# Layer 0's attention rebuilt: q and k in two float32r pieces, heads in four groups of 32 partitions, projections between the batches

## Chip, cores and metric

One core of one Trainium2 chip runs the whole two-layer block as one program. The metric is the device time of one execution in microseconds; the figure of the kernel before is the median of three runs.

## The reference, cut to what matters

There are 16 batches of 128 features by 256 positions. Only the first of the four blocks, layer 0's cross attention, is touched by the change. It has 16 heads of 8 features.

```
q = split(Wq @ layernorm(x) + bq)   k = split(Wk @ ctx + bk)   v = split(Wv @ ctx + bv)   # 16 heads of 8
scores = q^T k / sqrt(128)          attn = softmax(scores over the keys)                  # 256 x 256 for each head
x = x + tanh(g_xattn[0]) * (Wo @ (attn v) + bo)
```

The routed experts, the mLSTM, the second attention and its experts follow and need all 16 batches of x.

## The kernel before

Each engine has its instruction list written out by hand, and semaphores order them. In `layer0_*` the work on one head is two square score tiles: a maximum pass with the query on the partitions (`score_max`, L204, reduced by DVE at L423) and an exponential pass with the key on the partitions (`exponentials`, L232, ACT's exponential at L340). The negated maxima of a batch reach the second pass as extra rows of the contraction: PE turns them to rows, ACT and POOL split them, and SP copies them with a DMA into rows of `qs` (`max_rows`, L153).

Accuracy comes from q and k split in three bfloat16 pieces. All nine products of pieces stand below each other: 9 x 8 = 72 contraction rows, 75 with the maximum's three. SP builds that stack for a batch by storing the pieces in DRAM (`store_parts`, L132) and reading them back once for each product (`stack`, L146 and L147), into a ring of four batches (`A_RING`).

All projections, the split and the stores come first, for all 16 batches. Then 28 heads (`AHEAD`) of maxima run, and then a loop in which PE alternates maxima of head i + 28 with exponentials of head i. After every four heads (a group) `times_v` (L246) multiplies by v for four heads side by side, ACT copies the sums (L348), PE transposes them back (L256) and DVE divides (L430, L434). After a batch come two transposes, the output projection (L270), ACT's bias (L369) and DVE's add into x (L451). Banks: two for maxima, two for exponentials, two for `times_v`, one for the turn back, one for the batch's end.

SP's list is in order. In the main loop `stack(b + 4)` waits until the exponentials of batch b have been issued, and `max_rows(b + 2)` stands behind it:

```
        if n % A_PAIRS == A_PAIRS - 1 and n // A_PAIRS + A_RING < NB:
            stack(n // A_PAIRS + A_RING)
```

Of the kernel before, what the change touches and what calls it, by code (L numbers as in the profile page):

```python
# [11 lines left out]
ALU = mybir.AluOpType  # L12
# [61 lines left out]
QPART = (0, 0, 0, 1, 1, 1, 2, 2, 2)  # L74
KPART = (0, 1, 2, 0, 1, 2, 0, 1, 2)
TERM_ROWS = len(QPART) * HD
MAX_ROWS = 3
ROWS = TERM_ROWS + MAX_ROWS
TILES = 4
GROUPS = HEADS // TILES  # L80
A_PAIRS = HEADS // 2
A_SLOTS = 3
A_RING = 4
A_EXPS = 8
AHEAD = HEADS + 3 * HEADS // 4
A_STEPS = NB * A_PAIRS + 6


def layer0_memory(k, stack):
    sb = tensors(k, stack, "a")  # L90
    m = namedtuple("m", "wqT wkT wvT woT bias normed vaug whole parts qs ks negmax mrow mparts expo inv outq sumT outT proj stats mean_var rstd")
    return m(
        sb("wqT", [P, P]), sb("wkT", [P, P]), sb("wvT", [P, P]), sb("woT", [P, P]), sb("bias", [P, 4]),
        sb("normed", [P, NB, D]), sb("vaug", [P, NB, 2, HEADS, HD + 1]),
        [sb(f"whole{i}", [P, 2, BANK]) for i in range(A_SLOTS)], [sb(f"parts{i}", [P, 2, 3, BANK], BF16) for i in range(A_SLOTS)],
        [sb(f"qs{i}", [ROWS, HEADS, POS], BF16) for i in range(A_RING)], [sb(f"ks{i}", [96, HEADS, POS], BF16) for i in range(A_RING)],
        [sb(f"negmax{i}", [P, HEADS, 2]) for i in range(2)], [sb(f"mrow{i}", [32, P]) for i in range(2)],
        [sb(f"mparts{i}", [32, 3, P], BF16) for i in range(2)], [sb(f"exp{i}", [P, 2, POS]) for i in range(A_EXPS)],
        [sb(f"inv{i}", [P, 2, TILES]) for i in range(2)], [sb(f"outq{i}", [P, 2, HEADS, HD]) for i in range(2)],
        [sb(f"sumT{i}", [P, POS]) for i in range(2)], [sb(f"outT{i}", [P, POS]) for i in range(2)], [sb(f"proj{i}", [P, POS]) for i in range(2)],  # L100
# [4 lines left out]
def layer0_semaphores(k):  # L105
    s = k.sems("a", "weights_in var root normed qk_sums v_sums qk_whole qk_rounded q_rest k_rest q_middle k_middle q_low k_low v_copied k_ones "
               "max_scores maxed max_turned max_copied max_split exp_scores exped cleared weighted sums_copied turned_back divided "
               "out_sums out_turned proj_sums projected added")
    return s, {n: [k.sem(f"a_{n}{i}") for i in range(count)] for n, count in (("q_out", A_SLOTS), ("k_out", A_SLOTS), ("stack_in", A_RING), ("max_in", A_RING))}


def layer0_sp(k, m, s, ring):
# [7 lines left out]

    load_inputs(0)
    sp.dma_start(k.gates[:, :], io["gates"]).then_inc(k.gates_in, DMA)
    for dst, name in ((m.wqT, "a_wqT"), (m.wkT, "a_wkT"), (m.wvT, "a_wvT"), (m.woT, "a_woT"), (m.bias, "a_bias")):
        sp.dma_start(dst[:, :], io[name]).then_inc(s.weights_in, DMA)
    for chunk in range(1, NCHUNK):
        load_inputs(chunk)

    def store_parts(i):
        for n, (name, ready) in enumerate((("q", s.q_low), ("k", s.k_low))):
            sp.wait_ge(ready, i + 1)  # L130
            for j in range(2):
                sp.dma_start(io[f"a_{name}_parts"][2 * i + j].rearrange("t p n -> p t n"),  # L132
                             m.parts[i % A_SLOTS][:, n, :, j * POS:(j + 1) * POS]).then_inc(ring[f"{name}_out"][i % A_SLOTS], DMA)

    def stack(b):
        r, i = b % A_RING, b // 2
        flat = lambda t, first, count: t[first * HD:(first + count) * HD, :, :].rearrange("p h n -> p (h n)")
        parts_of = lambda n: io[f"a_{n}_parts"][b].rearrange("t (d h) n -> t d (h n)", d=HD)
        sp.wait_ge(ring["q_out"][i % A_SLOTS], 2 * DMA * (i // A_SLOTS + 1))
        sp.wait_ge(ring["k_out"][i % A_SLOTS], 2 * DMA * (i // A_SLOTS + 1))  # L140
        if b < A_RING:
            sp.wait_ge(s.k_ones, b + 1)
        else:
            sp.wait_ge(s.exp_scores, (b - A_RING + 1) * HEADS)
        for t in range(3):
            sp.dma_start(flat(m.qs[r], 3 * t, 3), parts_of("q")[t].unsqueeze(0).broadcast_to([3, HD, HEADS * POS])).then_inc(ring["stack_in"][r], DMA)  # L146
            sp.dma_start(flat(m.ks[r], 3 * t, 3), parts_of("k")).then_inc(ring["stack_in"][r], DMA)  # L147

    def max_rows(b):
        sp.wait_ge(s.max_split, b + 1)  # L150
        for part in range(MAX_ROWS):
            row = TERM_ROWS + part
            sp.dma_start(m.qs[b % A_RING][row:row + 1, :, :].rearrange("o h (q n) -> o (h q) n", q=2),  # L153
                         m.mparts[b % 2][:, part, :]).then_inc(ring["max_in"][b % A_RING], DMA)

# [2138 lines left out]
```

## Time and profile before

| | |
|---|---|
| median of 3 runs | 1817.8 us (1807.99 to 1822.12) |
| profiled execution | 1817.43 us, span 1816.1 us, mean granted clock 0.94 |
| layer 0's attention | 0 to 350.4 us of the span |
| PE, DVE, ACT, POOL busy in the span | 88%, 69%, 56%, 42% |
| DMA moved | 137.42 MB, mean 76 GB/s |

The busy shares are means over stages with different limits. The changed stage is the first fifth of the span; the stages behind it start when its last batch has been added to x.

### The profile page before, as it was taken

How to read it: one execution, taken by the hardware profiler on the slowest of the kernel's cores; microseconds unless marked ns; L12 is line 12 of the kernel's file. 1: busy time of each engine (PE TensorE's matmuls, PEld its weight loads, DVE VectorE, ACT ScalarE, POOL GpSimd, SP SyncE). 2: the span in 40 equal slices, each digit the busy share in tenths (PEclk: the TensorE clock that was granted, in tenths of full speed). 3: DMA queues.
4: the chain of work that ended last, by engine and by line, in shares of the span. 5: the costliest groups of instructions: out<-in, count | busy, mean ns of one | idle time of the engine just before them, and what ended most of it. 6: DMA issues, size and time to landing. Idle time of an engine off the chain costs nothing.

```text
span 1816.1 us, 30483 instructions
## 1 busy us (share of the span) xinstructions
PE 1606.5 (88%) x10932; PEld 1268.4 (70%) x10932; DVE 1259.6 (69%) x2321; ACT 1019.4 (56%) x2050; POOL 765.8 (42%) x575
## 2 busy tenths in 40 slices
PE   4379999789999999999986964899899999999898
PEld 2135555368888888888872533788787778888687
DVE  6458788378644455444445576999999999999454
ACT  4247777644433335333335653877776877677453
POOL 5200000024435333333330014798798688877000
PEclk9569899899999999999996987999999999999899
DMA  5613232243343333343400002123112111211220
GB/s 155 154 55 83 76 84 61 80 111 105 94 129 106 104 110 102 108 116 102 118 10 6 4 2 92 48 72 103 56 56 68 56 56 56 68 48 30 70 47 24
DMA packets 73349, 137.42 MB, mean 76 GB/s; under 512 B 12824, under 2 KB 41308, under 8 KB 70384
## 3 DMA queue, kind: packets, MB, share of 16 engines
q1 hardware_dynamic: 73200, 135.48, 26.4%
q8 instruction: 88, 1.44, 0.3%
q14 instruction: 61, 0.50, 0.1%
HBM read 125.70 MB, written 8.95 MB: 74 GB/s over the span
## 4 chain that ended last, share of the span: by engine, by line
PE 54%; DVE 19%; issue 9%; DMA 8%; ACT 6%; POOL 2%; SPq 1%; DVEq 0%; ACTq 0%; POOLq 0%
PE bank L67 13%; PE bank L69 13%; PE bank L68 13%; DMA a_qs<-a_mparts 5%; DVE b_straight L1938 3%; DVE b_straight L1892 2%; PE bank L246 2%; PE bank L232 2%; PE bank L204 2%; ACT b_turned L1809 2%; DVE b_peak L1909 2%; POOL e_hidden L944 1%; DVE b_probs L1907 1%; PE bank L1700 1%; PE bank L1732 1%
## 5 line engine op out<-in xcount | busy, mean ns | idle before, releaser
L944 POOL TENSOR_TENSOR e_hidden<-e_gated,e_comb_wide 128x512 f32<-128x512 f32 x132 | 211.0, 1599 | 346.7 <-DVE e_gated L909 331.1
L784 ACT CAST e_hidden_hi<-e_hidden 128x512 fp32r<-128x512 f32 x132 | 82.0, 622 | 320.6 <-POOL e_hidden L944 320.6
L902 DVE TENSOR_TENSOR e_hidden_lo<-e_hidden,e_hidden_hi 128x512 fp32r<-128x512 f32 x132 | 98.2, 744 | 209.8 <-ACT e_hidden_hi L784 209.8
L423 DVE TENSOR_REDUCE a_negmax<-bank 128x2 f32<-128x512 f32 x256 | 165.6, 684 | 64.6 <-PE bank L204 63.3
L69 PE MATMUL bank<-e_x_hi,e_weights_lo 128*128 128x512 f32 (+1 forms) x528 | 209.5, 397 | 0.0
L67 PE MATMUL bank<-e_x_hi,e_weights_hi 128*128 128x512 f32 (+1 forms) x528 | 208.4, 395 | 0.7 <-ACT e_comb_rows L744 0.7
L68 PE MATMUL bank<-e_x_lo,e_weights_hi 128*128 128x512 f32 (+1 forms) x528 | 208.4, 395 | 0.0
L1809 ACT ACTIVATE b_turned<-bank,b_swap_bias 64x512 f32<-64x512 f32 x256 | 174.9, 683 | 17.7 <-PE bank L69 12.9
L1996 POOL TENSOR_TENSOR b_turned<-b_turned,b_rope 128x512 f32<-128x512 f32 x128 | 167.5, 1329 | 5.3 <-ACT b_turned L1809 4.8
L340 ACT ACTIVATE a_exp<-bank 128x512 f32<-128x512 f32 x256 | 142.9, 596 | 42.8 <-PE bank L232 35.4
L69 PE MATMUL bank<-e_weights_hi,e_hidden_lo 128*128 128x256 f32 (+1 forms) x528 | 149.4, 283 | 0.0
L67 PE MATMUL bank<-e_weights_hi,e_hidden_hi 128*128 128x256 f32 (+1 forms) x528 | 148.2, 281 | 0.5 <-DVE e_hidden_lo L902 0.5
L68 PE MATMUL bank<-e_weights_lo,e_hidden_hi 128*128 128x256 f32 (+1 forms) x528 | 148.4, 281 | 0.0
L1938 DVE TENSOR_TENSOR b_straight<-b_straight,b_turned 128x512 f32<-128x512 f32 x128 | 140.5, 1136 | 0.0
L1798 ACT ACTIVATE b_probs<-b_probs,b_peak_scaled 128x128 f32<-128x128 f32 x256 | 99.7, 391 | 68.2 <-DVE b_peak_scaled L1911 68.1
L204 PE MATMUL bank<-a_ks,a_qs 72*128 72x256 bf16 x512 | 108.0, 297 | 31.0 <-DMA a_ks<-a_k_parts 13.2
L1978 POOL TENSOR_TENSOR b_qk_lo<-b_raw_qk,b_qk_hi 128x512 fp32r<-128x512 f32 x64 | 84.7, 1324 | 109.9 <-DVE b_qk_hi L1872 109.9
L909 DVE TENSOR_TENSOR e_gated<-e_silu,bank 128x512 f32<-128x512 f32 x132 | 90.5, 686 | 56.7 <-PE bank L69 44.2
L232 PE MATMUL bank<-a_qs,a_ks 75*128 75x256 bf16 x512 | 100.2, 280 | 21.0 <-DMA a_qs<-a_mparts 20.1
L69 PEld LDWEIGHTS bank<-e_x_hi,e_weights_lo 128*128 128x128 f32 (+1 forms) x528 | 98.7, 187 | 22.7
L67 PE MATMUL bank<-b_x_hi,b_qk_hi 128*128 128x512 f32 x256 | 103.0, 402 | 12.8 <-POOL b_qk_lo L1978 4.5
L67 PEld LDWEIGHTS bank<-e_x_hi,e_weights_hi 128*128 128x128 f32 (+1 forms) x528 | 99.4, 188 | 19.7 <-ACT e_comb_rows L744 1.1
(326 smaller groups left out, 4318.1 us busy)
## 6 DMA issues: line engine op xcount, KB each, us to landing
e_comb_wide<-e_combT SPq DMA_DIRECT2D x130, 256.0 KB, 4.0
e_raw<-in_e_weights SPq DMA_DIRECT2D x64, 384.0 KB, 4.5
b_raw_qk<-in_b_wqk SPq DMA_DIRECT2D x64, 256.0 KB, 2.8
a_qs<-a_q_parts SPq DMA_DIRECT2D x48, 192.0 KB
a_ks<-a_k_parts SPq DMA_DIRECT2D x48, 192.0 KB
b_raw_v<-in_b_wv SPq DMA_DIRECT2D x16, 512.0 KB, 3.8
b_raw_o<-in_b_wo SPq DMA_DIRECT2D x64, 128.0 KB, 2.0
moe_comb_wide<-b_comb_rows SPq DMA_DIRECT2D x16, 256.0 KB, 6.7
```

Source lines behind the costliest of these rows:

```text
L67: pe.matmul(out, w_hi, x_hi, start=start, stop=False, skip_group_check=True)
L68: pe.matmul(out, w_hi, x_lo, start=False, stop=False, skip_group_check=True)
L69: return pe.matmul(out, w_lo, x_hi, start=False, stop=stop, skip_group_check=True)
L204: last = pe.matmul(bank[:, qb * POS:(qb + 1) * POS], m.qs[r][0:TERM_ROWS, h, qb * P:(qb + 1) * P], m.ks[r][0:TERM_ROWS, h, :], start=True, ...
L232: last = pe.matmul(bank[:, kb * POS:(kb + 1) * POS], m.ks[r][0:ROWS, h, kb * P:(kb + 1) * P], m.qs[r][0:ROWS, h, :], start=True, stop=True)
L340: act.activation(m.expo[at % A_EXPS][:, :, :].rearrange("p k q -> p (k q)"), banks[2 + h % 2][:, :], ACT.Exp, scale=float(1 / np.sqrt(np.f ...
L423: dve.tensor_reduce(m.negmax[b % 2][:, h, :], banks[h % 2][:, :].rearrange("p (q n) -> p q n", q=2), AX.X, ALU.max, negate=True).then_inc( ...
L944: pool.tensor_tensor(m.hidden[i][0:rows, :], m.gated[i][0:rows, :], m.comb_wide[u % E_RING][0:rows, chunk * BANK:(chunk + 1) * BANK], ALU. ...
L1798: last = act.activation(w.probs[n % 3][:, b, :], w.probs[n % 3][:, b, :], ACT.Exp, scale=SCALE, bias=w.peak_scaled[i][:, b:b + 1], accum_o ...
L1809: last = act.activation(w.turned[i][dst:dst + half, which, :], banks[bank][src:src + half, :], ACT.Identity, bias=m.swap_bias[dst:dst + ha ...
L1938: dve.tensor_tensor(w.straight[n % 2][:, which, :], w.straight[n % 2][:, which, :], w.turned[n % 2][:, which, :], ALU.add).then_inc(s.rotated)
L1996: pool.tensor_tensor(x, x, w.rope[:, 1, :].unsqueeze(1).to_broadcast([P, CHUNK, S]), ALU.mult).then_inc(s.qk_sine)
```

## The change

- q and k become two float32r pieces (high, low) instead of three of bfloat16, and three products are kept: 24 contraction rows, 26 with two rows for the maximum. Heads are stacked in four groups (lanes) of 32 partitions, four heads in each; a matmul then uses 32 partitions of the array.
- Work is counted in slots of two heads; a batch is 8 slots, a pair of batches 16. One DVE instruction reduces both heads of a slot over two banks (1024 elements). The exponentials follow the maxima by `LEAD` = 15 slots (30 heads). Order on PE in a slot: exponential, maximum, exponential, three maxima, two exponentials.
- Only the first two pairs are projected ahead; the others are projected in slots 0, 2 and 4 of a pair (q, k, v), in banks of the maxima's ring (`USES`). The projections lose one ACT pass, the second rounding pass and POOL's passes: ACT writes the high piece, DVE the low one.
- Stores and stacks are made for a pair of batches at a time: six stores and eight stack DMAs. The ring holds three pairs. `stack(i)` for i of 3 and more waits for the exponentials of pair i - 3.
- POOL splits the maxima before the transpose, ACT copies the rows, SP places them with two DMAs.
- `times_v` and the turn back have one bank each, and the batch's end shares the bank of the turn back. ACT's bias pass at the end is gone: POOL adds the bias to x, and DVE adds the product from PSUM. The tanh of the gates and their load come later in the order.

```diff
-MAX_ROWS = 3
+A_TERMS, MAX_ROWS = 3, 2
+TERM_ROWS = A_TERMS * HD
 ROWS = TERM_ROWS + MAX_ROWS
+LANE, LANES = 32, 4
+TILES = LANES
+A_SLOTS = HEADS // 2
+A_PAIRS = NB // 2
+A_RING, A_PARTS, A_MAXIMA, A_EXPS = 3, 2, 4, 8
+LEAD = 15
+A_LAST = NB * A_SLOTS
+A_STEPS = A_LAST + LEAD + A_SLOTS
+TURN_AT, SPLIT_EVERY = A_SLOTS + 2, 2 * A_SLOTS
+SCORE_SLOTS = 2
+EXP_BANK, SUM_BANK, TURN_BANK = 4, 6, 7
...
+    i, at = t // SPLIT_EVERY + 2, t % SPLIT_EVERY
+    return ({0: "q", 2: "k", 4: "v"}[at], i) if at in (0, 2, 4) and i < A_PAIRS else None
...
+    uses = [(kind, i) for kinds in ("qk", "v") for i in range(2) for kind in kinds]
+    for t in range(A_LAST):
+        uses.append(("max", t))
+        if projection_of(t):
+            uses.append(projection_of(t))
+    return uses
...
+    def store(i):
+        sp.wait_ge(s.low, 2 * (i + 1))
+        both = lambda n, part: m.parts[i % A_PARTS][:, n, part, :].rearrange("p (j n) -> p j n", j=2)
+        for n, (dst, terms) in enumerate(((k.q_stack, (0, 0, 1)), (k.k_stack, (0, 1, 0)))):
+            for term, part in enumerate(terms):
+                sp.dma_start(dst[2 * i:2 * i + 2, term].rearrange("j p n -> p j n"), both(n, part).bitcast(F32)).then_inc(ring["stored"][i % A_PARTS], DMA)
+    def stack(i):
+        r = i % A_RING
+        sp.wait_ge(ring["stored"][i % A_PARTS], 2 * A_TERMS * DMA * (i // A_PARTS + 1))
+        if i < A_RING:
+            sp.wait_ge(s.ones, A_RING)
+        else:
+            sp.wait_ge(s.exp_scores, (i - A_RING + 1) * 2 * HEADS)
+        for src, dst in ((k.q_stack, m.qs), (k.k_stack, m.ks)):
+            for lane in range(LANES):
+                rows = src[2 * i:2 * i + 2].rearrange("j t (d g h) n -> t d g j (h n)", g=LANES, h=GROUPS)[:, :, lane].rearrange("t d j n -> (t d) j n")
+                sp.dma_start(dst[r][LANE * lane:LANE * lane + TERM_ROWS, :, :, :].rearrange("p j h n -> p j (h n)").bitcast(F32),
+                             rows).then_inc(ring["stack_in"][r], DMA)
+    def max_rows(b):
+        sp.wait_ge(s.max_copied, b + 1)
+        for part in range(MAX_ROWS):
+            rows = m.qs[b // 2 % A_RING][TERM_ROWS + part:P:LANE, b % 2, :, :].rearrange("g h n -> g (h n)").bitcast(F32)
+            sp.dma_start(rows, m.mrow[b % 2][LANE * part:LANE * (part + 1), :].bitcast(F32)).then_inc(ring["max_in"][b % A_MAXIMA], DMA)
     load_inputs(0)
...
+    for t in range(A_STEPS):
+        at, i = t % SPLIT_EVERY, t // SPLIT_EVERY + 2
+        if t % A_SLOTS == TURN_AT % A_SLOTS and TURN_AT <= t < A_LAST + TURN_AT:
+            max_rows((t - TURN_AT) // A_SLOTS)
+        if at == 5 and i < A_PAIRS:
+            store(i)
+        if at == 9 and i < A_PAIRS:
+            stack(i)
 
 
...
+    def freed(use):
+        at = USE[use] - SCORE_SLOTS
+        if at >= 0:
+            kind, i = USES[at]
+            if kind == "max":
+                pe.wait_ge(s.maxed, i + 1)
+            elif kind == "v":
...
+    def scores(t):
+        u = t - LEAD
+        maximum, exponential = t < A_LAST, 0 <= u < A_LAST
+        if exponential:
+            if u % A_SLOTS == 0:
+                b = u // A_SLOTS
+                pe.wait_ge(ring["max_in"][b % A_MAXIMA], MAX_ROWS * DMA * (b // A_MAXIMA + 1))
+            if u:
+                pe.wait_ge(s.exped, 2 * u - 1)
+            exp_pair(u, 0, 0)
+        if maximum:
+            if t % (2 * A_SLOTS) == 0:
+                i = t // (2 * A_SLOTS)
+                pe.wait_ge(ring["stack_in"][i % A_RING], 2 * LANES * DMA * (i // A_RING + 1))
+            freed(("max", t))
+            max_pair(t, 0, 0)
+        if exponential:
+            exp_pair(u, 0, 1).then_inc(s.exp_scores)
+        if maximum:
+            max_pair(t, 1, 0)
+            max_pair(t, 0, 1)
+            max_pair(t, 1, 1).then_inc(s.max_scores)
+        if exponential:
+            if u:
+                pe.wait_ge(s.exped, 2 * u)
+            exp_pair(u, 1, 0)
+            exp_pair(u, 1, 1).then_inc(s.exp_scores)
...
+    def turn_back(g):
+        b, h = divmod(g, GROUPS)
+        pe.wait_ge(s.sums_copied, g + 1)
+        if g:
+            pe.wait_ge(s.divided, g)
+        if b and h == 1:
+            pe.wait_ge(s.out_turned, b)
+        if b and h == 2:
+            pe.wait_ge(s.added, b)
...
+    def to_features(b):
+        pe.wait_ge(s.divided, min(GROUPS * (b + 1) + 1, GROUPS * NB))
...
+        pe.wait_ge(s.divided, min(GROUPS * (b + 1) + 2, GROUPS * NB))
+        pe.matmul(banks[TURN_BANK][:, 0:POS], m.woT[:, :], m.outT[b % 2][:, :], start=True, stop=True).then_inc(s.proj_sums)
...
+    for t in range(A_STEPS):
+        u = t - LEAD
+        scores(t)
+        if projection_of(t):
+            project(*projection_of(t))
+        if t % A_SLOTS == TURN_AT % A_SLOTS and TURN_AT <= t < A_LAST + TURN_AT:
+            max_to_rows((t - TURN_AT) // A_SLOTS)
+        if u % 2 == 0 and 2 <= u < A_LAST + 2:
+            times_v((u - 2) // 2)
+        if u % 2 and 3 <= u < A_LAST + 3:
+            turn_back((u - 3) // 2)
+        if u % A_SLOTS == 4 and u >= 12:
+            to_features(u // A_SLOTS - 1)
+        if u % A_SLOTS == 6 and u >= 14:
+            residual(u // A_SLOTS - 1)
...
+    def high(kind, i):
+        n = "qk".index(kind)
+        act.activation(m.parts[i % A_PARTS][:, n, 0, :], banks[score_bank((kind, i))][:, :], ACT.Identity, bias=m.bias[:, n:n + 1]).then_inc(s.high)
...
+    def maxima(t):
+        b = t // A_SLOTS
+        (lane, h), _ = heads_of(t)
+        first = score_bank(("max", t))
+        dve.wait_ge(s.max_scores, t + 1)
+        if b >= 2 and t % A_SLOTS == 0:
+            dve.wait_ge(s.max_split, b - 1)
+        dve.tensor_reduce(m.negmax[b % 2][:, lane:lane + 2, h, :], k.psum[:, first:first + 2, :].rearrange("p s (q n) -> p s q n", q=2), AX.X, ALU.max,
                           negate=True).then_inc(s.maxed)
...
+    def divide(g):
+        b, h = divmod(g, GROUPS)
+        view = banks[TURN_BANK][:, 0:2 * P].rearrange("p (q g d) -> p q g d", q=2, g=LANES)
+        dve.wait_ge(s.turned_back, g + 1)
...
+    for t in range(A_STEPS):
+        u = t - LEAD
+        if t < A_LAST:
+            maxima(t)
+        if t and projection_of(t - 1):
+            read(*projection_of(t - 1))
+        if u % 2 == 0 and 4 <= u < A_LAST + 4:
+            divide((u - 4) // 2)
+        if u % A_SLOTS == 7 and u >= 15:
+            b = u // A_SLOTS - 1
+            dve.wait_ge(s.proj_sums, b + 1)
+            dve.wait_ge(s.biased, b + 1)
+            dve.scalar_tensor_tensor(k.resid[:, b, :], banks[TURN_BANK][:, 0:POS], k.gates[:, 0:1], k.resid[:, b, :], ALU.mult, ALU.add).then_inc(s.added)
...
-        pool.wait_ge(s.max_copied, b + 1)
-        pool.tensor_tensor(m.mrow[i][:, :], m.mrow[i][:, :], m.mparts[i][:, 0, :], ALU.subtract).then_inc(own.tick())
+        negmax, (high, low) = m.negmax[b % 2][:, :, :, :].rearrange("p g h q -> p (g h q)"), (m.mparts[b % 2][:, part, :] for part in range(2))
+        pool.wait_ge(s.maxed, A_SLOTS * (b + 1))
+        if b >= 2:
...
+        pool.tensor_scalar(k.resid[:, b, :], k.resid[:, b, :], m.late_bias[:, 0:1], None, ALU.add).then_inc(s.biased)
```

## Rows read from the trace of the kernel before

**Rows 1.** Windows of layer 0's attention: engines' busy us (instructions), granted clock, DMA share, GB/s.
```profile
0.00:66.00 66.00, 29.35 (x100) 17.14 (x100) 37.82 (x80) 30.36 (x54) 32.07 (x24) 0.85 0.54 157
66.00:111.00 45.00, 16.40 (x56) 3.91 (x57) 20.44 (x32) 2.81 (x5) 4.68 (x6) 0.50 0.43 114
111.00:118.00 7.00, 7.00 (x41) 3.84 (x42) 3.46 (x5) 4.08 (x9) 1.11 (x3) 0.50 0.00 0
118.00:126.00 8.00, 8.00 (x80) 4.87 (x79) 6.62 (x14) 6.34 (x13) 0.00 (x0) 0.98 0.03 5
126.00:322.00 196.00, 185.91 (x1861) 111.08 (x1860) 156.10 (x330) 151.03 (x316) 14.50 (x39) 0.97 0.29 76
322.00:350.50 28.50, 24.27 (x221) 10.77 (x219) 6.58 (x24) 21.34 (x47) 1.11 (x3) 0.94 0.01 2
```

**Rows 2.** The chain of waits, 60 to 360 us: start, length, what.
```profile
96.28 14.61 DMA a_qs<-a_mparts
...
163.29 7.34 DMA a_qs<-a_mparts
```

**Rows 3.** Timeline of the attention's last instruction: start, length, engine, line.
```profile
349.93 0.48 DVE L451 SCALAR_TENSOR_TENSOR resid<-a_proj,gates,resid 128x256 f32<-128x256 f32 x1 [3.05 <-ACT a_proj L369]
```

**Rows 4.** Timeline of SP's DMA issues for one batch: start, length, issue.
```profile
154.34 0.75 SPq L146 DMA_DIRECT2D a_qs<-a_q_parts  x1
155.13 0.44 SPq L147 DMA_DIRECT2D a_ks<-a_k_parts  x1
...
162.05 1.19 SPq L153 DMA_DIRECT2D a_qs<-a_mparts  x2
```

**Rows 5.** Windows of three DMA stretches: columns as in the first group.
```profile
38.00:40.00 2.00, 1.94 (x9) 0.93 (x7) 0.98 (x2) 2.00 (x4) 1.27 (x2) 1.00 1.02 286
76.00:84.00 8.00, 2.42 (x8) 0.52 (x8) 3.22 (x6) 0.00 (x0) 0.00 (x0) 0.50 0.77 144
163.00:169.00 6.00, 6.00 (x65) 3.67 (x65) 5.07 (x13) 5.00 (x11) 0.00 (x0) 1.00 0.20 71
```

**Rows 6.** Groups of instructions, 110.9 to 350.5 us: count, busy us, mean ns, idle before.
```profile
L423 DVE TENSOR_REDUCE a_negmax<-bank 128x2 f32<-128x512 f32 x227 | 146.9, 684 | 50.0 <-PE bank L204 50.0
L340 ACT ACTIVATE a_exp<-bank 128x512 f32<-128x512 f32 x256 | 142.9, 596 | 42.8 <-PE bank L232 35.4
...
L348 ACT COPY a_sumT<-bank 128x256 f32<-128x256 f32 x64 | 23.8, 372 | 26.1 <-PE bank L246 26.1
...
L434 DVE TENSOR_TENSOR a_outq<-bank,a_inv 128x64 f32<-128x64 f32 x64 | 14.4, 225 | 2.2
L430 DVE RECIPROCAL a_inv<-bank 128x8 f32<-128x8 f32 x64 | 12.7, 199 | 17.2 <-PE bank L256 17.2
...
L451 DVE SCALAR_TENSOR_TENSOR resid<-a_proj,gates,resid 128x256 f32<-128x256 f32 x16 | 7.8, 484 | 6.6 <-ACT a_proj L369 6.6
```

**Rows 7.** Groups of DVE's instructions in later stages, shapes kept apart.
```profile
L1948 DVE SCALAR_TENSOR_TENSOR b_outT_lo<-bank,b_head_bias,b_outT_hi 128x512 fp32r<-128x512 f32 x64 | 47.2, 737 | 3.5 <-ACT b_outT_hi L1837 3.5
...
L1344 DVE TENSOR_REDUCE m_factor<-m_square 128x64 f32<-128x1024 f32 x4 | 4.8, 1210 | 0.0
```

**Rows 8.** Timeline of PE, one group of four heads.
```profile
120.31 1.05 PE L246 MATMUL bank<-a_exp,a_vaug 128*9 128x256 f32 x16
121.29 0.39 PE L204 MATMUL bank<-a_ks,a_qs 72*128 72x256 bf16 x2
121.52 0.39 PE L232 MATMUL bank<-a_qs,a_ks 75*128 75x256 bf16 x2
```

**Rows 9.** Timeline of PE in the mLSTM stage: matmuls of 32 partitions each.
```profile
1037.01 1.17 PE L1236 MATMUL bank<-columns,m_keys 32*128 32x128 f32 x32
```

**Rows 10.** Timeline of PE in the expert stage: float32r matmuls of 256 columns.
```profile
471.71 0.28 PE L68 MATMUL bank<-e_weights_lo,e_hidden_hi 128*128 128x256 f32 x1
471.82 0.28 PE L69 MATMUL bank<-e_weights_hi,e_hidden_lo 128*128 128x256 f32 x1
```

**Rows 11.** Timeline of a projection of 512 columns in the first stretch.
```profile
35.40 1.02 PE L186 MATMUL bank<-ctx,a_wkT 128*128 128x512 f32 x2
```

More of the change, by code:

```diff
@@ L124, in layer0_sp @@
         sp.dma_start(dst[:, :], io[name]).then_inc(s.weights_in, DMA)
+    sp.dma_start(k.gates[:, :], io["gates"]).then_inc(k.gates_in, DMA)
     for chunk in range(1, NCHUNK):
         load_inputs(chunk)
[L128 to L154, printed above, removed]
-    for i in range(1, NB // 2 + 1):
-        store_parts(i - 1)
-        if i == 3:
-            stack(0)
-    for b in range(1, A_RING):
-        stack(b)
-    for i in range(AHEAD):
-        if i >= 2 and (i - 2) % HEADS == HEADS - 1:
-            max_rows((i - 2) // HEADS)
@@ L165, in layer0_sp @@
[L165 to L171 removed]
+    for i in range(2):
+        store(i)
[5 more added lines that the diff above has]
+        if at == 5 and i < A_PAIRS:
+            store(i)
+        if at == 9 and i < A_PAIRS:
+            stack(i)
@@ new lines, in layer0_act @@
+    for chunk in range(1, NCHUNK):
+        root(chunk)
+    act.wait_ge(k.gates_in, DMA)
+    act.activation(k.gates[:, :], k.gates[:, :], ACT.Tanh).then_inc(k.gates_ready)
+    for t in range(A_STEPS):
+        u = t - LEAD
+        if t and projection_of(t - 1) and projection_of(t - 1)[0] in "qk":
+            high(*projection_of(t - 1))
+        if 0 <= u < A_LAST:
+            exponentials(u)
+        if t % A_SLOTS == TURN_AT % A_SLOTS and TURN_AT <= t < A_LAST + TURN_AT:
+            max_to_rows((t - TURN_AT) // A_SLOTS)
+        if u % 2 == 0 and 2 <= u < A_LAST + 2:
+            times_v((u - 2) // 2)
+        if u % A_SLOTS == 4 and u >= 12:
+            to_features(u // A_SLOTS - 1)
@@ new lines, in layer0_dve @@
+    norm_start(0)
+    dve.memset(m.vaug[:, :, :, :, HD], 1.0)
+    dve.memset(banks[SUM_BANK][:, :], 0.0).then_inc(s.cleared)
+    norm_end(0)
+    for kind, i in USES[:4]:
+        read(kind, i)
+    for chunk in range(1, NCHUNK):
+        norm_start(chunk)
+        if chunk == 1:
+            for i in range(2):
+                read("v", i)
+    for chunk in range(1, NCHUNK):
+        norm_end(chunk)
+    dve.wait_ge(s.weights_in, 5 * DMA)
+    dve.wait_ge(k.gates_ready, 1)
+    dve.tensor_tensor(m.late_bias[:, :], m.bias[:, 3:4], k.gates[:, 0:1], ALU.mult).then_inc(s.late_bias)
```

377 lines of the change are left out of this document (127 added, 250 removed).

## The prediction

> **What bounds the kernel now.** I read the windows first, to cut the attention out of the span: it ends at 350.4 us, and nothing behind it starts before [rows 1, 3]. So the change is worth what it moves that end. The stretches differ. To 66 us everything is projected, split and stored. From 66 to 111 us PE is 36% busy, at half its clock. The chain shows why: the first exponential needs the first rows of maxima, whose DMA landed 14.61 us after its issue, at 110.9 us [rows 2]. From 111 us the loop of two heads runs, with PE at 95%, DVE at 80% and ACT at 77% of 126 to 322 us [rows 1]. A group of four heads is 3.3 us from one `times_v` to the next where nothing is late, and PE takes 0.98 us of it for `times_v`, then 0.22 us for each pair of score matmuls [rows 8]. Once in every batch a wait on the maxima's DMA stands in the chain: 7.34 us from issue to landing for 16 KB [rows 2], because the batch's stack was issued 7.7 us ahead of it in the same queue [rows 4].
>
> **The transfers.** What the change does to them decides most. A stack DMA of today has 24 rows of 8 KB, in two kinds. Between 76 and 84 us, with both queued, 0.77 of 16 engines, about 12, moved 144 GB/s, 12 GB/s each; between 163 and 169 us 0.20, about three, moved 71 GB/s, 22 GB/s each [rows 5]. I read this as follows: the k stack, 24 plain rows, is spread over 12 engines, which get in each other's way; the q stack, three copies of eight rows, over three, and they make the tail. A store, with 128 partitions, used all 16 (share 1.02) at 286 GB/s [rows 5].
>
> The new stack is eight DMAs of the k kind: 24 rows x 2 x 4 KB = 197 KB each, 1.57 MB for a pair. At 144 GB/s that is 10.9 us; with 1.7 us before the first byte and 0.5 us after the last, 13 us from first issue to landing. If the four lanes kept twelve engines out of each other's way at 22 GB/s each, it would be 6.0 us, 8 us to landing. I take 13: the rows per DMA are today's, only the partition they start at moves. The store of a pair, 1.57 MB, takes 5.5 us, 7.5 to landing. SP's issue, 0.44 us each [rows 4], is less than either.
>
> The rows show the 12 and the 3 engines. The Trainium skill, "DMA: Bandwidth & Descriptors", section "Why a DMA increments its semaphore by 16 and not by 1", has the rule: the number of engines is the largest, up to 16, that divides the slowest dimension of both sides; 24 and 24 give 12, 24 and 3 give 3, and the trace agrees. "SBUF — State Buffer", section "Door 1: The DMA port swizzle", speaks against this change: 24 partitions reach six ports, and partitions 32 apart share them, so lanes 0 and 1 would gain nothing. By both, with 27 GB/s for a port, a stack would be 9.6 us by an estimate from those pages, against 10.9 by the row.
>
> **Until the first exponential** (now 110.9 us). x lands and is normalised with POOL's memset beside it; I put the low piece of k for pair 0 at 15 us (today the first store is issued at 27.9, behind a longer split). Store 0 lands at 23, stack 0 at 36, and maxima start. Store 1 queues behind it to 42, stack 1 to 55, store 2 (its projections run in slots 0 and 2) to 60, stack 2 to 73. `max_rows(0)` stands behind stack 2 on SP and in the queue: 73.5. PE reached slot 15 at about 57 (15 slots of 1.4 us) and waited. Gain 37 us; with stacks of 8 us instead of 13 the same list gives 58, a gain of 53.
>
> **The slot** (two heads). DVE: one reduce of 1024. The group that has this size takes 1.21 us [rows 7], and 512 take 0.68 [rows 6], 0.645 back to back; I take 1.18, 18.9 us for a pair's 16. Eight divisions at 0.38 (0.20 + 0.23, overlapped [rows 6]) 3.0, two adds of 0.48, the new reads of q, k, v, 0.74 [rows 7], 0.74 and 0.69: 2.1. Sum 25.0 us for a pair; today 32 x 0.645 + 3.0 + 1.0 = 24.6. The halved instruction count is paid out again for the projections. ACT: 32 exponentials at 0.585, eight copies at 0.37, two outputs at 0.47, rows 0.4, two high pieces 1.2: 24.2, against 24.4 with the bias passes. PE: 16 x 8 score matmuls at 0.109 are 14 us today. In the mLSTM stage 32 records of 0.107 us in rotating lanes took 1.0 us [rows 9], so lanes overlap almost fourfold; the order of a slot here is a c a d c d b b, two per lane in four turns of 0.118 (the float32r pace [rows 10]), 0.47 us: 7.5 us a pair. Added: three projections, 0.86 to 1.0 each [rows 11], 2.8 us, and a drain of about 0.2 us at each change between lanes and the whole array, some 5 us a pair. With `times_v` 7.8, transposes and outputs 5, PE comes to about 28 against today's 26. So all three engines stay near 25 us for a pair and none is freed. Today that runs at 27.6 (13.8 us a batch without a stall), 1.72 a slot.
>
> Two things are added. A projection takes a place in the maxima's two-place ring, so the next maxima wait for a reduce and, a slot later, for the low piece to be read: six small gaps of 0.2 us. And the one bank of the turn back makes PE wait three times a batch for DVE inside the same slot: `to_features` for the division that stands behind `maxima(t)`, `residual` for another, and the turn back after it for the add; behind each are the next slot's scores, which ACT and DVE want. I charge 0.9 us a batch. That makes 1.87 a slot with projections (slots 15 to 96, 82 of them: 153), 1.72 without (31: 53), and 1.5 for the last 15, which have no maxima (today the last 14 took 22 us after 322 [rows 1]): 22. Sum 229 us. With every engine's gaps gone it would be 195 (25.0 / 16 = 1.56); with the lanes not overlapping and the waits in full, 255.
>
> **The stall that is added.** `stack(m + 2)`, for m of 1 to 5, waits until PE has issued the last exponential of pair m - 1, in slot 16 m + 14. `max_rows(2m)` stands behind it on SP, and the first thing PE does in slot 16 m + 15 is to wait for those rows. Its maxima were ready four slots earlier. So PE stands from the end of one slot until SP has issued ten DMAs and the queue has moved 1.57 MB: 13 us less 0.9 of PE's other work, 12.1. Everything is queued behind that wait: the slot's maxima, `times_v`, the turn back; DVE and ACT run dry. Then the clock: after the wait before 110.9 us PE ran at 0.50 (1.2 GHz) for 7 us and did 41 matmuls, against 80 in 8 us at 0.98 [rows 1], so 2.9 us are lost. Five times 15.0 is 75 us. With 8 us stacks it is five times 8, 40. POOL's split ahead of the transpose and the two copies in place of three are hidden by two slots; odd batches have a free queue.
>
> **The end.** From the last exponential to the add 6.6 us today; less ACT's bias, 0.49: 6.1.
>
> **The sum.** 73.5 + 3 (slow clock after the first wait) + 229 + 75 + 6 = 386.5 us, against 350.4: +36. The profiled execution took 1817.4 us, the median is 1817.8, so no correction is needed: 1853 us.
>
> **The rivals.** First, the one on the other side: the lanes keep the transfers apart. One mechanism moves both startup and stalls: 58 + 2 + 229 + 40 + 6 = 335, 1802 us, and with a slot of 1.8 instead of 1.87 1796. It decides below 8.5 us from first issue to landing. For it: partitions in four places, half the packet size. Against: the 144 GB/s are those of 24 rows in flight, whatever follows them in the queue. Second: a stack of 10 to 11 us, partly apart, gives 1827, no change to be measured. Third: the lanes do not overlap, or the drains cost more. PE would need 35 us a pair, 2.15 a slot with projections and 1.85 without, 255 in place of 229: 1879. Against it is the mLSTM's row [rows 9], whose order of lanes is a plain rotation, for it that this order comes back to a lane after one other. The Trainium skill, "TensorEngine Tiling (Array Packing)", section "Tiling Modes", says that a change of tiling mode drains the engine; no row here prices it. Fourth, the change does not do what I say: the rows of maxima overtake the stack in the queue, and the stall is only SP's ten issues, about 6 us: -30, 1823. Today's 7.34 us speak against it.
>
> **How the numbers follow.** My forecast has 0.45, the third rival 0.10 (both slower), the second and fourth 0.22 together, the first 0.18, and 0.05 stays for a slot much nearer 1.56 (34 us less). Runs of this kernel spread by about 1% around their median, so 1% is what can be told from no change: slower over 1% 0.55, within 1% 0.23, faster 0.22. The range is 1787 to 1885: from the first rival with a slot of 1.75, to the third with part of both.
>
> **What would show each step.** First exponential near 73 us (58 if the first rival holds). DMA share near 0.75 at about 145 GB/s while a stack runs. Five waits of PE on the DMA of `a_mrow` of about 12 us, 32 heads apart, and a clock of 0.5 after each. DVE's reduce near 1.2 us. 1.85 us a slot between stalls. It is wrong if a stack lands within 8 us, if the slot is below 1.7, or if the waits are put down to another engine.

## The result, and the profile after

The changed kernel takes **1901.2 us** (median of 4 runs, 1887.4 to 1915.4) against 1816.0 for the kernel before: a ratio of **1.047**, 95% interval 1.038 to 1.056. The profiled execution has a span of 1901.9 us (1816.1 before). The direction was forecast, the size was not: 1901 is above the range. In what follows, medians and ratios leave out runs more than 1.5% above the fastest of the same kernel (one of `e2_dve_order`, one of `e4_no_projections`, four of `e7_divide_first`).

Windows of the attention in the changed kernel; columns as in [rows 1]:

```profile
56.00:64.00 8.00, 2.38 (x12) 1.50 (x12) 4.73 (x5) 0.00 (x0) 0.00 (x0) 0.50 0.68 142
64.00:96.00 32.00, 28.52 (x262) 14.66 (x262) 22.15 (x30) 20.96 (x42) 2.74 (x6) 0.81 0.16 51
96.70:100.00 3.30, 0.41 (x2) 0.20 (x2) 1.54 (x2) 0.96 (x2) 0.00 (x0) 1.00 0.54 129
100.00:104.00 4.00, 0.00 (x0) 0.00 (x0) 0.00 (x0) 0.00 (x0) 0.00 (x0) 0.51 0.79 173
...
170.00:220.00 50.00, 33.36 (x292) 16.61 (x288) 24.62 (x36) 22.45 (x46) 2.74 (x6) 0.69 0.25 64
...
320.00:370.00 50.00, 42.37 (x383) 21.07 (x376) 30.91 (x47) 28.67 (x59) 4.11 (x9) 0.72 0.01 3
```

Against [rows 1] two columns stand out: the granted clock, 0.97 in the loop before, is 0.66 to 0.81 here, and from 320 us on, behind the last projection and the last stall, it is still 0.72. Timeline of PE at the first exponential (here and below: the first of PE's score matmuls for it), and of DVE at the attention's last instruction, which answers to [rows 3]:

```profile
64.12 0.57 PE L241 MATMUL bank<-a_qs,a_ks 26*128 26x256 f32 x1 [4.81 <-DMA a_qs<-a_mrow]
...
422.76 0.48 DVE L490 SCALAR_TENSOR_TENSOR resid<-bank,gates,resid 128x256 f32<-128x256 f32 x1 [1.79 <-PE bank L317]
```

The first exponential is at 64.1 us (111 before), yet the attention ends at 423.2 (350.4 before). So its loop takes 359 us in place of 239. PE's waits, 0 to 440 us (engine, line, waited for, total us, times, longest):

```profile
PE bank L241 <- DMA a_qs<-a_mrow: 53.5, 6, 10.0
PE bank L305 <- DVE resid L490: 24.1, 14, 1.8
...
PE bank L311 <- DVE a_outq L459: 7.8, 9, 1.5
```

The first is the stall of every pair, the others are waits inside the slots: of `turn_back` (L305) for the residual addition and of `to_features` (L311) for the division. The chain of waits through a stall, which answers to [rows 2, 4]:

```profile
92.51 2.41 DVE a_negmax L448 x2
94.92 0.12 DVE a_inv L455
95.07 0.23 DVE a_outq L459
95.31 0.14 issue
95.44 0.67 PE bank L317 x2
96.11 0.31 PE bank L241
...
96.71 0.32 SPq L172
...
100.88 7.51 DMA a_qs<-a_mrow
108.44 0.58 PE bank L241
```

First a small wait: DVE does two maxima, then the division, and only then can PE go on with `residual` (L317) and the scores behind it. Then the stall: SP's eight issues of the stack (from 96.71), the rows of maxima behind them, PE idle until 108.44. From one such stall to the next it is 51 us (SP's stacks are issued at 145.0, 196.0, 247.2 and 298.4 us), of which PE waits 9.7: 2.6 us for each of 16 slots, where the forecast gives 2.05 (1.87, and 2.9 us of half clock over 16). Groups of instructions, 64 to 423 us, against [rows 6]:

```profile
L366 ACT ACTIVATE a_exp<-bank 128x512 f32<-128x512 f32 x256 | 138.9, 594 | 130.3 <-PE bank L241 129.3
L448 DVE TENSOR_REDUCE a_negmax<-bank 128x4 f32<-128x1024 f32 x113 | 138.1, 1225 | 153.3 <-PE bank L234 153.0 <-POOL a_mparts L511 0.2
```

Neither DVE nor ACT is the bound: each sits idle about as long as it works, waiting for PE.

### The profile page after: what moved, and what is told of

It is laid out like the page before. It is cut to its first block, busy times and chain, and to the rows that moved or that the text cites. A ratio compares the mean times of both kernels' runs of the same rounds, so it can differ in the third digit from the quotient of the medians.

```text
span 1901.9 us, 30248 instructions
## 1 busy us (share of the span) xinstructions
PE 1638.8 (86%) x10932; PEld 1271.2 (67%) x10932; DVE 1243.3 (65%) x2193; ACT 990.0 (52%) x1985; POOL 739.4 (39%) x558
## 4 chain that ended last, share of the span: by engine, by line
PE 58%; DVE 20%; issue 8%; ACT 5%; DMA 5%; SPq 2%; POOL 1%; DVEq 0%; POOLq 0%; ACTq 0%
PE bank L68 12%; PE bank L70 12%; PE bank L69 12%; PE bank L241 4%; PE bank L283 4%; DVE b_straight L1972 3%; DMA a_qs<-a_mrow 2%; DVE a_negmax L448 2%; DVE b_straight L1926 2%; ACT b_turned L1843 2%; DVE b_peak L1943 2%; PE bank L1734 1%; DVE b_probs L1941 1%; PE bank L1766 1%; POOL e_hidden L978 1%
## 5 line engine op out<-in xcount | busy, mean ns | idle before, releaser
L448 DVE TENSOR_REDUCE a_negmax<-bank 128x4 f32<-128x1024 f32 x128 | 155.7, 1224 | 165.0 <-PE bank L234 164.7
L366 ACT ACTIVATE a_exp<-bank 128x512 f32<-128x512 f32 x256 | 138.9, 594 | 130.3 <-PE bank L241 129.3
L241 PE MATMUL bank<-a_qs,a_ks 26*128 26x256 f32 x512 | 104.0, 411 | 56.5 <-DMA a_qs<-a_mrow 53.5
L241 PEld LDWEIGHTS bank<-a_qs,a_ks 26*128 26x128 f32 x512 | 68.7, 245 | 111.5 <-DMA a_qs<-a_mrow 55.0
```

Of the source, the lines that this page charges most:

```text
L241: return pe.matmul(banks[EXP_BANK + side][:, kb * POS:(kb + 1) * POS], m.ks[r][rows, b % 2, h, kb * P:(kb + 1) * P], m.qs[r][rows, b % 2, ...
L366: act.activation(m.expo[at % A_EXPS][:, :, :].rearrange("p k q -> p (k q)"), banks[EXP_BANK + side][:, :], ACT.Exp, scale=float(1 / np.sqr ...
L448: dve.tensor_reduce(m.negmax[b % 2][:, lane:lane + 2, h, :], k.psum[:, first:first + 2, :].rearrange("p s (q n) -> p s q n", q=2), AX.X, A ...
```

## The experiments

The tables give the median, the ratio to the kernel before, and from each profile the first exponential, the end of the attention and the time between ("loop"). The kernel before was run again beside each set of runs, and its median there was 1824.1 us (e1 to e4), 1821.4 (e5 to e8), 1815.3 (e9 to e12) and 1820.3 us (e13 to e16), so that across sets it is the ratios that compare. Positions and clocks are those of one profiled execution of each kernel.

### Which of the two kinds of wait

`e1_stack_late`, in SP's list:

```
-        if at == 9 and i < A_PAIRS:
+        if at == 15 and i < A_PAIRS:
             stack(i)
```

> The stack of a later pair is issued by SP in slot 16m+15 and no longer in slot 16m+9, so the row transfer of slot 16m+10 is no longer queued behind it. Theory A (the stalls, and the half clock after each, are most of the miss): the six waits of PE for a_mrow, 53.5 us in all, vanish, the granted clock between 70 and 320 us rises from 0.66-0.80 to 0.9 or more, the attention ends about 70 us earlier than 423 us, and the time is near 1830 us. Theory B (the clock falls for another reason, the waits inside the slots or the 32-row matmuls): the 53.5 us go, the clock stays between 0.65 and 0.8, and the time is near 1850 us. Theory C (the transfer still gets in the way): the odd batch's row transfer, issued three slots behind the stack, lands late in its place; the waits for a_mrow only move, at least 30 us of them stay, and the time is over 1870 us.

`e2_dve_order`, in DVE's list (the residual addition moves up in the same way):

```
-        if t < A_LAST:
-            maxima(t)
         if t and projection_of(t - 1):
             read(*projection_of(t - 1))
         if u % 2 == 0 and 4 <= u < A_LAST + 4:
             divide((u - 4) // 2)
         ...
+        if t < A_LAST:
+            maxima(t)
```

> In each slot DVE does the division and the residual addition ahead of the maximum, not behind it; nothing else moves and the six stalls stay. Theory C2 (the waits inside the slots count): the 24.1 us in which PE waits in turn_back for the residual addition and the 16.3 us in to_features for the division mostly go, as both are now ready before PE asks; the maxima start up to 0.7 us later in every second slot, which is hidden; the attention ends 25 to 40 us earlier and the time is 1860 to 1875 us. Rival: PE only waits for the later maximum instead, the attention ends within 10 us of 423 us and the time is within 1% of 1901 us.

`e3_both` has both edits.

> Both edits together. If the stalls and the waits inside the slots are all that was missed (theory A), the slot comes down from about 2.35 us with stalls to about 1.8 us, the granted clock is 0.95 or more from 70 us on, the attention ends near 320 us and the time is near 1795 us, below the 1816 us of the kernel before. If the clock is low for a reason of its own (theory B), it stays under 0.85, the slot stays above 2 us, the attention ends after 340 us and the time is 1820 us or more.

| | median us | ratio (95%) | first exp. | end | loop |
|---|---|---|---|---|---|
| after | 1901.2 | 1.047 (1.038-1.056) | 64.1 | 423.2 | 359 |
| e1_stack_late | 1839.7 | 1.008 (1.005-1.011) | 59.1 | 362.1 | 303 |
| e2_dve_order | 1836.4 | 1.011 (1.003-1.020) | 64.0 | 364.6 | 301 |
| e3_both | **1753.8** | **0.961** (0.958-0.964) | 55.9 | 287.2 | 231 |

Windows of `e1_stack_late`:

```profile
120.00:170.00 50.00, 40.77 (x366) 20.29 (x364) 30.99 (x46) 28.70 (x60) 2.74 (x6) 0.75 0.25 66
```

Windows of `e3_both`:

```profile
33.00:56.00 23.00, 18.10 (x74) 10.59 (x74) 17.86 (x17) 1.63 (x3) 1.36 (x3) 0.50 0.68 188
...
170.00:220.00 50.00, 45.65 (x523) 24.19 (x523) 42.54 (x66) 39.20 (x80) 5.45 (x12) 1.00 0.40 98
220.00:270.00 50.00, 46.30 (x501) 24.08 (x497) 33.80 (x57) 39.84 (x84) 4.09 (x9) 1.00 0.02 4
```

Each edit alone wins some 61 to 65 us, both together 147. That is more than the sum, but not by more than the noise: in the ratios the two take off 3.9 and 3.6 points and both together 8.6, and the 1.1 points over the sum are no wider than the intervals. What shows that the two faults meet is the clock. With the stalls gone it stayed at 0.69 to 0.76 from 120 us on, as theory B said (the median, 1840 us, lies halfway between the two theories). In e2 it was 0.78 to 0.86. With both gone it is 1.00 from 70 to 270 us, as theory A said, and the attention ends at 287 us where 320 was expected. So matmuls of 24 and 26 rows don't rule the full clock out, and what share pauses and matmuls have in the low one is for the later runs. In e2 the six stalls even grew, to 64.9 us. The order of DVE alone (e2) was worth more than its expectation, 1860 to 1875 us. `e3_both` beats both kernels.

### Which of the small waits

Two steps between e1 and e3: `e6_read_first` (only DVE's `read` ahead of `maxima`) and `e7_divide_first` (`read` and `divide`).

> On top of the stack in slot 16m+15, only DVE's reads of the projected banks go ahead of the maximum; division and residual addition stay behind it. These touch 18 of the 143 slots, and PE's waits for them were 5.0 us together: 0 to 10 us less than 1840 us, the clock stays near 0.76.

> On top of that the division too goes ahead of the maximum; the residual addition stays behind it. PE's waits for the division (to_features 8.2 us, residual 7.4 us between 70 and 360 us) vanish, the wait for the addition (24.1 us, 14 times) stays. If the clock follows each pause, two of the three pauses of a batch are gone and two thirds of the 86 us between this and the kernel with all three orders go: near 1785 us, clock 0.85 to 0.9. If only the waits themselves count, 16 us go: near 1820 us. If the one long pause that is left is enough to keep the clock down, it stays under 0.8.

Medians 1829.3 and 1810.3 us, ratios 1.005 and 0.992; loops of 295 and 281 us, so the ladder from e1 to e3 is 303, 295, 281, 231. PE's waits in `e7_divide_first`, 70 to 340 us:

```profile
PE bank L305 <- DVE resid L490: 23.8, 13, 1.8
```

This last wait, 1.8 us once in a batch and 23.8 us in all, is worth 50 us of loop (e7 to e3; some 3 points of the ratio). The clock in e7 was between 0.97 and 0.67 by stretch; without that wait it was 1.00. My first theory (two thirds of the gain, 1785 us) fell, and 1820 was nearer.

### Pauses or the kind of matmul

A matmul of full height here has 128 rows of contraction, a low one 32 or fewer.

`e5_filler` keeps e1's waits and puts work into two of them:

```
+    def filler(count):
+        for _ in range(count):
+            pe.matmul(banks[SUM_BANK][:, POS:2 * POS], m.wqT[:, :], m.normed[:, 0, :], start=True, stop=True)
 ...
+        if b and h == 2:
+            filler(4)
         if g:
             pe.wait_ge(s.divided, g)
 ...
+        if u % A_SLOTS == 4 and 12 <= u < A_LAST:
+            pe.wait_ge(s.sums_copied, (u - 2) // 2)
+            pe.wait_ge(s.max_copied, min(((u - 2) // 2 + 3) // GROUPS + 1, NB))
+            filler(3)
```

> The kernel with the stack in slot 16m+15, all its waits inside the slots in place, and seven extra matmuls (128 rows, 256 columns, into an unused half of the sums' bank) in each batch, put ahead of two of the three places where PE waits for DVE: four ahead of the transposes of turn_back that wait for the residual addition, three in the slot of to_features. Theory A (PE's pauses of 1 to 2 us are what keeps its clock down): the pauses are filled, the granted clock between 70 and 320 us rises from 0.69-0.76 to over 0.9, and the kernel gets faster by 15 to 35 us than the 1840 us without the extra work, though PE does 112 more matmuls of 0.43 us each at the full clock. Theory B (the clock is low for the kind of matmuls, 24 or 26 rows of the array, or for the mixture): the clock stays under 0.8 and the time stays or grows, 1840 to 1880 us.

`e15_filler_narrow` is the same with operands of 32 rows, `m.wqT[0:LANE, :]` and `m.normed[0:LANE, 0, :]`.

> The kernel of the filler experiment (1809 us, clock 1.00 from 70 to 320 us) with its seven extra matmuls of a batch over 32 rows and not 128; PE's pauses are filled for the same time. Theory A (the pauses alone lower the clock): 1809 us and 1.00 again. Theory B2 (the height counts too): the clock falls between 0.7 and 0.95 and the time is 1815 to 1850 us.

| | median us | ratio (95%) | first exp. | end | loop |
|---|---|---|---|---|---|
| e1_stack_late | 1839.7 | 1.008 (1.005-1.011) | 59.1 | 362.1 | 303 |
| e5_filler (128 rows) | 1808.8 | 0.992 (0.990-0.996) | 59.6 | 336.5 | 277 |
| e15_filler_narrow (32 rows) | 1869.1 | 1.028 (1.022-1.033) | 59.8 | 404.5 | 345 |

Windows of `e5_filler`:

```profile
120.00:170.00 50.00, 46.08 (x461) 26.25 (x459) 34.04 (x52) 31.65 (x65) 4.11 (x9) 1.00 0.36 89
```

Windows of `e15_filler_narrow`:

```profile
120.00:170.00 50.00, 47.87 (x350) 25.50 (x339) 26.25 (x39) 24.23 (x50) 2.73 (x6) 0.64 0.24 65
```

With 105 matmuls more (the traces have them; the expectation counted 112), PE finished 26 us earlier, and its clock was 1.00 in place of about 0.75. The same matmuls at a quarter of the height did the opposite, and by more than the 1815 to 1850 us expected: PE was busier still, its clock 0.64 to 0.74 between 120 and 370 us, and the loop took 68 us longer than with the full ones. Busy PE time alone doesn't hold the clock up.

Does it bring it back? In `e10_projections_first` the projections of all pairs stand ahead of the first maximum.

> Both edits (stack late, DVE's order), and all eight pairs are projected, split and stored ahead of the first maximum, as in the kernel before, instead of between the batches. If the projections between the batches are what the gain over the kernel before comes from, the first exponential goes from 55.9 us to 80 to 95 us (the stores of six more pairs stand ahead of the first maximum), the slots lose the projections' 15 to 20 us, and the time is 10 to 25 us over 1754 us. Rival (the two halves cancel, as PE's work is only moved): within 5 us of 1754 us.

1794.7 us, ratio 0.984 (0.978 to 0.991), 41 us over e3 where 10 to 25 were expected; first exponential 87.0, loop 240 us. Its clock was 0.50 from 76 to 142 us, with PE 99% busy in the last 50 of these. `e13_burst_full` and `e14_burst_narrow` add to e10 eight matmuls in one slot, over 128 and over 32 rows:

```
         scores(t)
+        if u == 4:
+            pe.wait_ge(s.max_copied, 2)
+            for _ in range(8):
+                pe.matmul(banks[SUM_BANK][:, POS:2 * POS], m.wqT[0:P, :], m.normed[0:P, 0, :], start=True, stop=True)
```

> The kernel with all projections first (1795 us; clock 0.50 from 76 to 142 us, though PE was 96 to 100% busy from 92 us on), and in the slot of the fifth exponentials eight extra matmuls of 128 rows by 256 columns, some 7 us at half clock. Theory B2 (a busy PE alone doesn't bring the clock back, matmuls over all 128 rows do; the loop's own are mostly 24 or 26 rows high or 9 columns wide): the clock is at 1.0 within the burst or a few us behind it, near 105 us, and 15 to 25 us go from 1795 us. Theory A2 (only how long PE has been busy counts, and it was 50 us there): the clock comes back near 142 us as before and the time is 1795 us plus 0 to 7.

> The same with the eight extra matmuls over 32 rows of the array and not 128: the same columns and the same time on PE. Theory B2: the clock stays at 0.50 until about 142 us or later, 1795 us plus 0 to 7. If this burst brings it back as the full one does, it is not the height of the matmuls.

Windows of `e13_burst_full`:

```profile
92.00:98.00 6.00, 6.00 (x44) 3.62 (x45) 3.96 (x6) 3.73 (x9) 0.96 (x2) 0.50 0.64 135
98.00:104.00 6.00, 6.00 (x36) 4.26 (x39) 0.65 (x1) 0.48 (x2) 0.00 (x0) 0.77 0.02 5
104.00:110.00 6.00, 5.46 (x68) 2.77 (x68) 5.15 (x8) 5.06 (x10) 0.00 (x0) 1.00 0.01 1
```

Windows of `e14_burst_narrow`:

```profile
98.00:104.00 6.00, 6.00 (x30) 3.21 (x28) 0.00 (x0) 0.01 (x1) 0.00 (x0) 0.50 0.00 0
...
140.00:170.00 30.00, 29.58 (x212) 14.56 (x213) 16.65 (x25) 15.92 (x33) 1.36 (x3) 0.50 0.02 6
170.00:220.00 50.00, 47.40 (x476) 24.17 (x475) 37.20 (x58) 35.56 (x73) 5.46 (x12) 0.82 0.29 65
```

In e13 the clock came back within the burst, at about 101 us (the burst ran from 97.7 to 102.9). Behind the low one it stayed at 0.50 until after 180 us, though PE was 99% busy. The medians, 1788.4 and 1792.5 us, don't tell the two apart, and 15 to 25 us were expected from the full burst; the profiled loops are 225 and 254 us, but e14's profiled execution, 1808 us, was the slowest of its four. The clock also comes back without any burst, at 142 us in e10 and after 180 in e14, so this pair alone is weak. Stronger are e5 against e15, whose runs lie over 46 us apart, and the pair e12 and e16 below.

### What a stall costs, and the head

`e9_stall_filler` is e2 with 24 full-height matmuls ahead of each wait for `a_mrow`.

> DVE's order as in the second experiment, the stack still in slot 16m+9, so PE still waits six times for a_mrow (64.9 us there, 1847 us); ahead of each of these waits PE gets 24 extra matmuls of 128 rows by 256 columns (0.43 us each at the full clock, 10.4 us together) into an unused half of a bank. The row transfers land no earlier. Theory A (the half clock after a stall costs as much as the prediction charged, 2.9 us for each): the clock between 70 and 320 us rises from 0.78-0.86 to 0.95 or more and 15 to 25 us go, 1822 to 1832 us. Rival: the clock falls for other reasons than the stall or costs nothing there, since DVE sets the pace of the slots: no change within 10 us.

Ratio 1.003 (1.000 to 1.006) against e2's 1.011 (1.003 to 1.020), clock 1.00 from 70 to 320 us. First exponential 68.5 (PE held up by the filler), end 352.2. The five later stalls were as long in both: 57.1 us of waiting in e2 (64.9 - 7.8), 52.6 us of filler and 4.8 us of waiting left in e9. The loops were 301 and 284 us. So the half clock after a stall costs 17 / 5 = 3.4 us, from one trace of each.

`e8_warm_start` is e3 with 22 such matmuls in PE's first wait for a stack; `e12_head_filler` puts 33 there and one into each of the first 17 slots; `e16_head_narrow` is e12 with 32 rows.

> Both edits (stack late, DVE's order), and 22 extra matmuls of 128 rows by 256 columns on PE in the 13.8 us in which it waits for the first stack. They should bring the granted clock, 0.50 from the start to about 60 us, to 1.0 before the first maxima. Theory: slots 0 to 14 have only maxima and are then paced by DVE's 1.2 us in place of PE's half-clock work, and the first slots with exponentials run at once at the full clock: 4 to 10 us less than 1754 us. If the start is bound by DVE and by transfers: no change within 3 us.

> Both edits, 33 extra matmuls (128 rows by 256 columns) in the wait for the first stack, 4.4 us more than in the warm start before, which had left a pause of 4.4 us and the clock at 0.50 behind it, and one such matmul in each of the first 17 slots. Theory: without the pause the first maxima run at the full clock, and with the extra matmul in each slot it stays there; slots 0 to 8 and the first exponential slots take less, and 4 to 10 us go from the 1754 us. Rival: PE is held up by the extra work or the head is paced by DVE and the transfers: no change within 3 us. If the clock still is 0.50 from 34 to 60 us, pauses are not what keeps it down there.

> The kernel of the head filler (1751 us, clock 1.00 from 33 us on) with its 33 + 17 extra matmuls over 32 rows and not 128. Theory A: no change, 1.00 from 33 us on, 1751 us. Theory B2: the clock is 0.50 at 33 us as it was without them, and comes back at about 65 us, with the projections of slots 16 to 20: 1751 to 1760 us, told apart by the clock and not by the time.

Medians 1759.2, 1750.7 and 1767.5 us; ratios 0.966, 0.963 and 0.973 against e3's 0.961, so neither e8 nor e12 gained the 4 to 10 us expected beyond noise. In e8 a pause of 4.4 us was left behind the filler, and the first maxima ran at 0.50. Windows of `e12_head_filler`:

```profile
33.00:56.00 23.00, 22.06 (x123) 12.14 (x122) 20.00 (x19) 2.90 (x6) 1.36 (x3) 1.00 0.73 200
```

Windows of `e16_head_narrow`:

```profile
22.00:23.00 1.00, 1.00 (x6) 0.85 (x6) 0.93 (x7) 0.15 (x1) 0.00 (x0) 1.00 0.52 123
26.00:33.00 7.00, 7.00 (x18) 5.50 (x17) 3.24 (x12) 0.49 (x2) 0.00 (x0) 0.50 0.92 227
33.00:56.00 23.00, 22.19 (x64) 13.54 (x64) 7.25 (x7) 1.38 (x2) 0.00 (x0) 0.50 0.51 133
```

PE is as busy in both, the clock is 1.00 and 0.50. In e16 PE began the low fillers at 18.9 us at the full clock and was 100% busy with them, and yet the clock fell to 0.50 between 23 and 24 us. There was no pause and no other matmul between, so the height is all that differs from e12. The clock came back at about 77 us, not 65, and the fillers, at half clock, put the first exponential off to 68.5 us: hence 1767.5 us where 1751 to 1760 were expected. The attention ends at 283.2 us in e12, 4 before e3; the ratio, 0.963 (0.958 to 0.968), can't be told from e3's.

### Two that moved nothing

> Both edits, and from the third pair of batches on q, k and v are not computed: no projections, splits or stores, and the stacks load the first two pairs' values again, so the scores of the later batches are those of the first four. Theory A prices the projections at PE's own work, 18 times about 0.85 us plus their waits for the bank, some 15 to 20 us less than the kernel with both edits, and puts nothing on the clock. If DVE's and ACT's reads of the projected banks hold the alternating score bank back, 30 us or more go and every pair of slots takes what a pair without projections took in the changed kernel, 3.1 us.

> Both edits, and in each slot PE does both heads' exponential scores first and the four maxima matmuls behind them, so ACT gets its second bank earlier; PE then waits for ACT's exponential of the slot before at a place where less of its own work lies ahead. If ACT's waits for scores (23.5 us between 0 and 440 us) are what is left, up to 10 us go from 1754 us; if PE's waits for ACT (32.8 us, 104 times) grow, as the banks of the exponentials are single, 10 to 40 us are added. The second is the likelier.

1753.9 and 1757.6 us, ratios 0.960 (0.955 to 0.966) and 0.965 (0.960 to 0.969), neither to be told from e3's 0.961 (0.958 to 0.964); 15 to 20 us less and, as the likelier, 10 to 40 us more had been expected. In e4's profiled execution, its slowest (1775 us), the clock was 0.50 until about 124 us, so what leaving out the projections (matmuls of 128 rows) saved may have gone into that; the price of the projections is not settled by it. In e11 the slot's order of matmuls made no difference to be measured: PE was 91% busy either way.

## Why the prediction was wrong

**The sum, term by term.** The attention was to end at 386.5 us and ended at 423.2.

| term | predicted | measured |
|---|---|---|
| first exponential | 73.5 | 64.1 |
| waits of the five later stalls | 60.5 | 48.7 (53.5 - 4.8) |
| everything else: slots, half clock after stalls, end | 252.5 (3 + 229 + 14.5 + 6) | 310.4 |

The start and the stalls were right in kind and 9 and 12 us too dear; **the step that failed is the slot**, by 58 us. The later stages, taken as unchanged, took 1478.7 us against 1465.7; with the same code behind other attentions they took 1463.2 (e9) to 1482.8 us (e4), and I have not found a cause for this spread.

**The slot term, where it held.** 229 + 6 = 235 us for 128 slots and the end was close to e3's loop (231), in part by luck: 14 of the 229 were for waits that e3 has not, so the rest was some 10 us too cheap. A pair took 28.9 us in e3 (94.34 to 123.28 us, and the next two alike), in which DVE's 25 us were 24.5, ACT's 24 were 22.5 and PE's 28 were 26.1; the reduce took 1.22 us. The third rival is out: lanes do overlap, a slot's eight score matmuls took 0.51 us at the full clock (171.88 to 172.39 us in e3), for 0.47 predicted. The 0.107 us that I gave each record of [rows 9] is not in those rows; the records there are 0.27 us long in the median. No run prices the drain of 0.2 us by itself. And the 195 us for slots without gaps should have been 198 (113 x 1.56 + 22).

**Where it failed: two charges in it.** I charged 0.9 us a batch for the waits of the turn back's bank, 14 us in all. The waits themselves were 2.8 us a batch (in e1 23.8 + 7.6 + 7.4 us between 70 and 340 us), because each stands behind a whole reduce of 1.22 us, PE's list is serial, and the scores behind it are what DVE and ACT wait for. And I took PE's clock as full outside the 7 us after a stall, from the loop before [rows 1], where PE was 95% busy with score matmuls of 72 and 75 rows [rows 8]. Here they have 24 and 26 and there are pauses among them; the clock fell, and the loop's own matmuls did not bring it back for tens of us. Whether the loop before, with its higher bfloat16 matmuls, would have borne the same pauses is not shown. Of the 72 us between e1's loop and e3's, for which the prediction had 14, 26 went when two of the pauses were filled at full height (e5, clock 1.00) and 46 are the waits, with the fillers in them. The prediction listed the clock as a cost of long stalls; it was a property of the whole loop.

**The transfers.** A stack took 11.8 us from first issue to landing (21.3 to 33.1; from 96.71 to 108.4 with the rows of maxima behind it), for 13 predicted, so neither the first rival (8) nor quite the row of before. It is 9.6 us net of the 1.7 and 0.5 us that I had put around it. That is the figure that my estimate from the Trainium skill, "SBUF — State Buffer", section "Door 1: The DMA port swizzle", had given: lanes 32 partitions apart share their ports. The trace agrees roughly: 1.57 MB in 9.6 us is 164 GB/s, and between 100 and 104 us 0.79 of the engines moved 173 GB/s, a little more than the 163 that six ports of 27.2 give, an estimate from that page. The fourth rival is out: the rows of maxima landed behind the stack each time. The six waits, their places and the 0.50 behind each were as forecast (9.7 us each of the later five for 12.1, and in e2 and e9 3.4 us of half clock for 2.9), and one line of SP's list removed them, which I had not asked of a change that I called a stall.

**The rivals' gap.** All four kept the clock. None was "the loop runs at a lower clock throughout", and by e5's 26 us that was nearly half of the 58 us missed in the slots; the waits, priced at a third of their length, were the rest. The Trainium skill, "TensorE: Matmul & The Clock Gate", section "A second HAM failure mode: psum-queue depth-cycling", says that frequent small idle times between groups of matmuls let the clock swing. e1 and e5 agree (0.75 and 1.00); e15 and e16 show what that section doesn't speak of, the height of the matmuls.

**Where the change's gain is.** e3 ends the attention 63 us before the kernel before: 55 from the first exponential (55.9 for 110.9), the rest from the loop (231 for 239). With the projections first (e10) 31 us of the earlier start were gone.

## What to carry to other kernels

A wait inside the innermost slot is not priced by its length: look behind which long instruction the releaser stands in its own engine's list, and move the short one ahead (here 72 us of loop for three calls reordered, 50 of them for the last). When a loop is made of low matmuls, price it at both granted clocks, and read the clock column of every stretch before you use a duration from it. Two faults that each hold the clock down hide one another: undo them together before judging either.

## What the runs showed of the hardware

- At the full clock and 100% busy with matmuls of 32 rows by 256 columns from 18.9 us on, PE fell to a granted clock of 0.50 (1.2 GHz) between 23 and 24 us (e16); with the same matmuls over 128 rows it kept 1.00 (2.4 GHz, e12).
- With PE 99% busy on matmuls of 24 and 26 rows, on 9-column ones, on short transposes and on one of 128 rows by 256 columns a batch, the clock stayed at 0.50 from 104 to 180 us (e14). In one trace eight matmuls of 128 rows by 256 columns brought it to 1.00 within their 5.2 us (e13).
- Pauses of 0.8 to 1.8 us, up to three in each batch of some 19 us, went with 0.69 to 0.76 (e1); two of the three filled at full height gave 1.00 (e5), filled at 32 rows 0.64 to 0.74 (e15). Without them (e3) the same loop kept 1.00 with PE at 91%.
- At 1.00 a pause of 4.4 us left 0.50 behind it (e8).
- The time at which a busy loop of low matmuls gets the full clock back is not fixed: after some 50 us at 0.50 with PE 99% busy in e10 (142 us), after more than 80 in e14 (between 180 and 190 us).
